# Two transformer layers on one core: whole-tile probability slots, 128-row tiles with a stacked tail in the first feed-forward product, and new due times

## The reference, cut to what matters

```python
def _layer(x, wqkv, qs, ksc, wo, lg, lb, w1, b1, w2, b2):
    h = shift_token(x)
    q, k, v = split(h @ wqkv)                  # 8 heads of 64
    q, k = rotary_xpos(l2norm(q) * qs, l2norm(k) * ksc)
    o = local_attention(q, k, v)               # window 128: own and previous 128 keys
    x = x + o @ wo
    h = layernorm(shift_token(x)) * lg + lb
    a, g = split(h @ w1 + b1)                  # 2 x 682 columns
    x = x + (a * gelu(g)) @ w2 + b2            # HID = 682
```

## Time and profile before

| what | value |
|---|---|
| median of 3 runs | 2306.94 us (2294.31 to 2309.14) |
| profiled execution | 2307.74 us, its span 2305.5 us |
| PE busy | 2047.1 us, 89% of the span |
| DVE busy | 1714.5 us, 74% |
| POOL busy | 1532.9 us, 66% |
| ACT busy | 1315.3 us, 57% |
| mean granted TensorE clock | 0.945 |

### The profile page before, as it was taken

The page is one execution under the profiler, slowest core; times in us unless marked ns, Lnnn a source line. Parts: engine busy times, 40 slices in busy tenths (PEclk is TensorE's granted clock), DMA queues, the critical chain, the costliest instruction groups (busy, mean ns, idle before and its releaser), DMA issues. The chain is left out here.

```text
span 2305.5 us, 45315 instructions
## 1 busy us (share of the span) xinstructions
PE 2047.1 (89%) x15360; PEld 1606.3 (70%) x15360; DVE 1714.5 (74%) x3132; ACT 1315.3 (57%) x3178; POOL 1532.9 (66%) x1401
## 2 busy tenths in 40 slices
PE   6579999999899999999998788979998989899985
PEld 4467777777677777777777576767676767677764
DVE  5587777677777887777676248888788788888883
ACT  3356566656665676567665356555655556456541
POOL 2465566556645755666465128988888789888984
PEclk7789999999999999999999889999999999999998
DMA  8343333333333333333333206777678767777685
GB/s 271 102 100 93 92 87 77 94 88 94 76 93 91 99 91 91 88 89 77 80 91 81 91 25 151 184 197 196 163 187 204 182 165 195 203 179 180 177 206 140
DMA packets 189280, 298.18 MB, mean 129 GB/s; under 512 B 52265, under 2 KB 97149, under 8 KB 188029
## 3 DMA queue, kind: packets, MB, share of 16 engines
q1 hardware_dynamic: 171388, 254.91, 43.1%
q10 hardware_dynamic: 10752, 21.51, 3.7%
q0 software_dynamic: 6912, 18.89, 3.2%
HBM read 56.04 MB, written 20.97 MB: 33 GB/s over the span
## 5 line engine op out<-in xcount | busy, mean ns | idle before, releaser
L2043 POOL TENSOR_TENSOR g_ring<-g_ring,g_rl 128x768 f32<-128x768 f32 (+6 forms) x168 | 384.8, 2304 | 40.7 <-DVE g_rl L1984 35.8
L1872 ACT ACTIVATE g_ring<-ps,g_mx 128x128 f32<-128x128 f32 (+7 forms) x384 | 274.2, 727 | 200.3 <-DVE g_mx L1966 92.2
L1759 PE MATMUL ps<-g_turned,g_latV 128*64 128x256 f32 (+1 forms) x1984 | 294.3, 442 | 73.6 <-issue 40.5
L855 ACT ACTIVATE l_pp<-ps,l_mx 128x256 f32<-128x256 f32 (+1 forms) x512 | 229.2, 464 | 169.0 <-DVE l_mx L992 169.0
L1131 POOL TENSOR_TENSOR l_pp<-l_pp,l_rl 128x1024 f32<-128x1024 f32 (+1 forms) x128 | 229.8, 1796 | 88.4 <-DVE l_rl L1000 88.2
L1991 DVE STREAM_TRANSPOSE g_ring<-g_ring 128x896 f32<-128x896 f32 (+4 forms) x264 | 257.2, 998 | 13.8 <-POOL g_ring L2043 13.5
L1759 PEld LDWEIGHTS ps<-g_turned,g_latV 128*64 128x64 f32 x1984 | 149.4, 143 | 162.9 <-issue 99.3
L1148 POOL TENSOR_TENSOR l_act_lo<-l_u,l_act_hi 114x512 fp32r<-114x512 f32 x96 | 125.5, 1307 | 162.4 <-ACT l_act_hi L905 162.2
L992 DVE CUSTOM_DVE_ANT_0 ps<-ps,l_mask 128x256 f32<-128x256 f32 (+1 forms) x512 | 188.4, 443 | 7.8 <-PE ps L704 7.8
L110 PE MATMUL ps<-l_wqkv_hi,l_x_hi 128*128 128x512 f32 x384 | 168.0, 437 | 17.9 <-POOL l_x_lo L1101 12.9
L110 PE MATMUL ps<-l_h_hi,l_w_hi 128*114 128x512 f32 (+1 forms) x384 | 160.7, 418 | 25.0 <-DVE l_h_lo L1049 22.2
(11 more groups left out here) (201 smaller groups left out, 6251.0 us busy)
## 6 DMA issues: line engine op xcount, KB each, us to landing
l_pt<-l_bt SPq DMA_DIRECT2D x1024, 64.0 KB, 2.0
g_turned<-g_ring SPq DMA_DIRECT2D x192, 112.0 KB, 3.0
g_turned<-g_ring SPq DMA_DIRECT2D x140, 128.0 KB, 3.8
g_turned<-g_pt SPq DMA_DIRECT2D x140, 128.0 KB, 3.5
g_turned<-g_ring SPq DMA_DIRECT2D x184, 96.0 KB, 2.9
g_turned<-g_ring SPq DMA_DIRECT2D x192, 80.0 KB, 2.4
g_turned<-g_pt SPq DMA_DIRECT2D x96, 96.0 KB, 2.2
l_tab<-turns SPq DMA_DIRECT2D x64, 128.0 KB, 2.1
```

Of the source, the lines that this page charges most:

```text
L855: act.activation(PP[:, i % NP, at, 0:n], ps[:, bank + a, jj * 2 * P:jj * 2 * P + n], ACT.Exp, bias=mx[:, g % 2, h, at:at + 1], scale=-1.0, ...
L1759: last = pe.matmul(o, latV[:, b % 2, c, :], turned[:, :, a, c, :, :], start=(c == 0), stop=(c == t), skip_group_check=True)
L1872: act.activation(to, some, ACT.Exp, bias=mx[:, u % 2, at:at + 1], accum_out=sm[:, u % 2, at:at + 1]).then_inc(s["ex"], 1)
L2043: pool.tensor_tensor(view, view, some, ALU.mult).then_inc(s["scaled"], 1)
```

## The change

Three edits in `layers`, and a new table.

1. `l_pp` and `l_bt` go. In their place there is `l_pb` with two slots, each of a whole tile. `exps` writes the probabilities in the order of the blocks, `scale` and `blocks` work in place. `exps` of tile `g` now waits, once, for the DMAs of `move(g-2)`; `blocks` waits for `scale` alone.
2. The feed-forward's tiles have 128 columns, so of 682 there are five full tiles and a rest of 42. The rests of both halves stand in one stationary operand (columns 0 to 41 and 64 to 105, zeros between), so the first product's last tile is one product of six matmuls into one bank, and the first product has 11 tiles where it had 12. In the second product the rest's high part stands in rows 0 to 41 and its low part in rows 64 to 105, over two copies of the 42 rows of `w2`, so that each of its two output halves takes two matmuls where it took three. The low part of the rest is written by DVE (`tail`), no longer by POOL.
3. The pieces of `w1` are split in two parts each (640 columns and the rest), the last piece of `w2` has its rest loaded and split twice, and three small memsets blank the padding.
4. All of `DUE` is new, but for the `bring` rows.

```diff
-HW = -(-HID // HT)
+HW = P
 HREM = HID - (HT - 1) * HW
+HMAIN = (HT - 1) * HW
+UPPER = slice(DH, DH + HREM)
...
-        PP = sb("l_pp", [P, NP, 4, 2 * P])
-        BT = sb("l_bt", [P, NB, 2, 4, 2, SQ])
+        PB = sb("l_pb", [P, 2, NB, 2, 4, 2, SQ])
...
                 def up(q, j, bank):
...
+                    if j == HT - 1:
+                        f = slice(2 * HMAIN, 2 * HMAIN + DH + HREM)
+                        three(pe, ps[0:DH + HREM, bank, :], [(W1_hi[:, k, f], W1_lo[:, k, f], hh[:, k, :], hl[:, k, :])
+                                                             for k in range(KD)]).then_inc(s["upg"], 1)
+                        return
...
                 def down(q, j, bank):
...
-                    pe.wait_ge(s["ulo"], n + 1)
+                    if j == HT - 1:
+                        pe.wait_ge(s["tail"], q + 1)
+                    else:
+                        pe.wait_ge(s["ulo"], (HT - 1) * q + j + 1)
...
+                        if j == HT - 1:
+                            pe.matmul(ps[:, bank + m, :], W2_hi[0:DH + HREM, j, f], ah[0:DH + HREM, j % NA, :], start=False,
+                                      stop=False)
+                            last = pe.matmul(ps[:, bank + m, :], W2_lo[0:mj, j, f], ah[0:mj, j % NA, :], start=False, stop=True)
...
                 def exps(g, h, bank):
...
-                    if i >= NP:
-                        act.wait_ge(s["blocks"], i - NP + 1)
...
                     if g >= 2:
                         act.wait_ge(s["rl"], i - 3)
+                        if h == 0:
+                            act.wait_ge(s[f"pt{g % 2}"], MOVED * (g // 2))
...
                 def blocks(g, h):
...
-                    if g:
-                        dve.wait_ge(s[f"pt{(g - 1) % 2}"], MOVED * ((g + 1) // 2))
-                    dve.transpose(BT[:, :, h, :, 0:n // P, :].rearrange("p j a r q -> p a r j q"),
-                                  PP[:, i % NP, :, 0:n].rearrange("p a (r j q) -> p a r j q", j=NB, q=SQ)
-                                  ).then_inc(s["blocks"], 1)
+                    view = PB[:, g % 2, :, h, :, 0:n // P, :].rearrange("p j a r q -> p j a (r q)")
+                    dve.transpose(view, view).then_inc(s["blocks"], 1)
...
+                def tail(q):
+                    j = HT - 1
+                    dve.wait_ge(s["uhi"], HT * (q + 1))
+                    dve.tensor_tensor(ah[UPPER, j % NA, :], u[0:HREM, j % 2, :], ah[0:HREM, j % NA, :], ALU.subtract
+                                      ).then_inc(s["tail"], 1)
...
-            "split": -12.69, "norm": -11.35, "var": -3, "gate": (-2.44, -1.97, -1.53, -1.48, -1.23, -0.63),
-            "scale": (-9.75, -9.39)},
+            "split": -12.19, "norm": -11.15, "var": -3.11, "gate": (-2.17, -2.0, -1.52, -1.23, -1.11),
+            "scale": (-9.93, -9.87)},
```

More of the change, by code:

```diff
@@ L407 @@
+            "store": -20.4, "move": -28.59},
         "pe": {
-            "proj": -3.66, "val": -3.55, "turn": -2.22, "scores": (-1.88, -1.86), "weigh": 0.45, "wo": 4.61,
-            "mean": 5.08, "var": 5.31, "centre": 5.44, "up": (5.8, 5.92, 6.16, 6.59, 6.6, 7.04),
-            "down": (6.61, 7.05, 7.37, 7.82, 7.87, 8.09)},
+            "proj": -3.73, "val": -3.46, "turn": -2.32, "scores": (-1.91, -1.87), "weigh": 0.43, "wo": 4.37, "mean": 4.99,
+            "var": 5.23, "centre": 5.37, "up": (5.87, 6.0, 6.14, 6.6, 6.72, 7.03),
@@ L411 @@
+            "down": (6.65, 7.04, 7.29, 7.72, 7.8, 7.94)},
         "act": {
-            "split": -3.96, "proj": -3.23, "norm": -2.43, "val": -2.47, "turn": -1.76, "divide": 1.05, "mean": 5.63,
-            "var": 5.68, "centre": 5.89, "up": (6.24, 6.53, 6.74, 6.99, 7.05, 7.38),
-            "gate": (6.43, 6.63, 7.04, 7.18, 7.73, 8.04), "scores": (-1.28, -1.05)},
+            "split": -4.02, "proj": -3.19, "norm": -2.61, "val": -2.94, "turn": -1.95, "divide": 0.98, "mean": 5.5,
+            "var": 5.64, "centre": 6.0, "up": (6.38, 6.5, 6.64, 6.95, 7.18, 7.28),
@@ L415 @@
+            "gate": (6.6, 6.62, 6.74, 7.11, 7.92, 7.96), "scores": (-1.27, -1.08)},
         "dve": {
-            "bring": (-45.53, -20.84, -5.06, -2.53, -1.95, -1.58, 2.75, 6.91, -3.84, -3.8, -3.51, -3.49, 2.47,
-             2.76, 3.67, 3.72, 5.21, 5.57, 6.42, 6.8), "scores": (-1.3, -1.26), "proj": -3.03, "turn": -1.62,
-            "wo": 5.26, "mean": 5.44, "centre": 5.92, "up": (6.38, 6.54, 6.85, 7.06, 7.26, 7.66), "out": 8.55,
-            "share": (-1.14, -0.81), "blocks": (-0.51, -0.45), "divide": 1.32, "low": 5.98},
+            "bring": (-45.53, -20.84, -5.06, -2.53, -1.95, -1.58, 2.75, 6.91, -3.84, -3.8, -3.51, -3.49, 2.47, 2.76,
+               3.67, 3.72, 5.21, 5.57, 6.42, 6.8), "scores": (-1.32, -1.3), "proj": -3.08, "turn": -1.79, "wo": 4.99,
@@ L420 @@
+            "mean": 5.39, "centre": 5.89, "up": (6.22, 6.54, 6.84, 6.96, 7.23, 7.63), "out": 8.52, "share": (-1.18, -1.05),
+            "blocks": (-0.83, -0.45), "divide": 1.43, "low": 5.92, "tail": 8.19},
         "pool": {
-            "split": -12.69, "norm": -11.35, "var": -3, "gate": (-2.44, -1.97, -1.53, -1.48, -1.23, -0.63),
-            "scale": (-9.75, -9.39)},
+            "split": -12.19, "norm": -11.15, "var": -3.11, "gate": (-2.17, -2.0, -1.52, -1.23, -1.11),
+            "scale": (-9.93, -9.87)},
@@ L524, in layers @@
                        "chi clo wo xw xcol mean hc hsq var ve vl vr vn vn2 vn3 rs rsb hn hhi hlo upg upa ge u uhi ulo "
-                       "dn y out whi wlo")
+                       "dn y out whi wlo pad tail")
         def place_of(g):
@@ L773, in down @@
                         f = slice(m * P, (m + 1) * P)
[L774 to L775 removed]
+                        if j == HT - 1:
+                            pe.matmul(ps[:, bank + m, :], W2_hi[0:DH + HREM, j, f], ah[0:DH + HREM, j % NA, :], start=False,
+                                      stop=False)
+                            last = pe.matmul(ps[:, bank + m, :], W2_lo[0:mj, j, f], ah[0:mj, j % NA, :], start=False, stop=True)
+                        else:
+                            last = three(pe, ps[:, bank + m, :], [(W2_hi[:, j, f], W2_lo[:, j, f], ah[:, j % NA, :],
+                                                                   al[:, j % NA, :])], start=(j == 0), stop=False)
                     last.then_inc(s["dn"], 1)
@@ L893, in up @@
                     if j >= 2:
-                        act.wait_ge(s["ulo"], n - 1)
-                    act.activation(u[0:mj, j % 2, :], ps[0:mj, bank, :], ACT.Gelu, bias=b1c[0:mj, q // (B * NC), 1, j:j + 1]
+                        act.wait_ge(s["ulo"], (HT - 1) * q + j - 1)
+                    rows = UPPER if j == HT - 1 else slice(0, mj)
+                    act.activation(u[0:mj, j % 2, :], ps[rows, bank, :], ACT.Gelu, bias=b1c[rows, q // (B * NC), 1, j:j + 1]
                                    ).then_inc(s["ge"], 1)
@@ L1068, in _ @@
                 dve.memset(xw[:, 1, 0:1], 0.0).then_inc(s["xcol"], 1)
+                blank = slice(2 * HMAIN + HREM, 2 * HMAIN + DH)
+                for some in (W1_hi[:, :, blank], W1_lo[:, :, blank], W2_hi[32:DH, HT - 1, :]):
+                    dve.memset(some.bitcast(F32), 0.0).then_inc(s["pad"], 1)
+                dve.wait_ge(s["pad"], 3)
                 for e in flow.program["dve"]:
@@ L1091, in _ @@
                         low(e[1])
+                    elif e[0] == "tail":
+                        tail(e[1])
                     elif e[0] == "up":
```

82 lines of the change are left out of this document (40 added, 42 removed).

## The result

| | median us | lowest to highest | runs |
|---|---|---|---|
| before | 2306.24 | 2294.31 to 2314.13 | 20 |
| changed | 2293.13 | 2283.0 to 2309.97 | 20 |

The ratio is 0.9946, with a 95% interval of 0.993 to 0.9963: 12 to 13 us less, where 27.6 were forecast. Timed once more beside the experiments, the changed kernel had 0.9974 (0.9954 to 0.9994). I compare the experiments with the middle of the two, 0.996 (9 us), and keep in mind that the two differ by 0.003, which is 7 us.

The account below looks back on a forecast made before the run. PE was taken to bound the layers' steady part, busy 95% of it, with short waits around the layer norm. The terms -29.6 - 3 + 0 + 0 + 3 + 2 = -27.6 us, from 2306.94, gave 2279 us, range 2255 to 2303.

Parts of the forecast that it names:

- rival (a): Layer norm: ACT's and DVE's chain sets the period, half or more of 29.6 us returns as PE waits; 2293 us, 28%.
- Its term for the clock: Steady chunks: 73.0 us at granted clock 1.00, 77.0 at 0.96; a fall in half of them costs up to 32 us.
- The matmuls, -29.6: Feed-forward, last `up` and `down` tiles: 8 fewer matmuls in each of 16 chunks, 0.231 us each, 29.6 us off PE.
- The new order, 0: Around the layer norm: bank wait (13.1 us) goes, wait for the centred chunk grows by as much; 0 together.
- The probabilities in place, -3: Layers' attention: instruction prices unchanged, DVE's 14.9 us wait for DMAs before `blocks` goes; 3 us gained.
- The tail, 0: DVE's subtraction ahead of `l_qk_lo`: 0.69 to 3.3 us each, hidden by the `down` matmuls; 0, uncovered 53 us.
- The bank of the last `up` tile, +3: Last `up` tile takes a `turn` bank pair, cover fits by 0.2 us; 3 us cost, between 0 and 19.
- The start, +2: Before 185 us: two subtractions per `w1` piece and a longer POOL memset; 2 us cost, from 0 to 13.
- The second layer's pieces, 0: Second layer's `w1` pieces, split in two, lie beside full PE work; no cost.
- the 1.8 us of a chunk: Sign of a right forecast: a steady chunk of the layers shorter by about 1.8 us.
- the 953 us of the large attention: Sign of a right forecast: the large attention, left alone by the change, as long as before, 953 us.
- The sign for (a): Sum of PE's waits in the layers higher by 15 us or more, or steady granted clock below 0.97.

Follow-up runs that it names:

- the probabilities alone: The kernel before with only the probabilities in place, on its own due times (0.9985) and on the new ones with a sixth gate time (1.0049).
- the old table: The changed kernel on the due times of the kernel before, five POOL gate times and 8.2 for the tail: 2303.59 us, ratio 1.0004.

## Why the prediction was wrong

The forecast of 2279 us was 14 us too low. The value is that of rival (a), 2293, but by luck: its mechanism, half or more of the 29.6 us coming back as waits, is only a part of what happened. In a pair of chunks 2.15 us of the 3.7 were gained; 0.90 went because the remaining matmuls cost more, 0.65 as idle time of PE. Its term for the clock was also misread: the two chunks of the earlier trace rows are not of one kind but an odd and an even one, which differ by 1.0 us at the full clock (72.88 and 73.86), and a fall of the clock, which takes a chunk's mean from 1.00 to 0.98, costs 1.55 us; 0.96 is two of them. Eight more falls are 12 us, not 32. By the prediction's own steps:

- **The matmuls, -29.6.** The price of 0.231 us is right where PE sets the pace: 12 matmuls put back cost 2.76 us. The step that failed first is the price of the part in `down`. "I price a narrow one of 106 columns like the others" looked at the columns; the tail's `down` has operands of 42 and 106 *rows* in turn, and with the scores behind them four matmuls took 3.09 us where six had taken 3.10. Instead of 16 x 0.46 = 7.4 us this is nothing. Equal rows bring the starts from 0.37 to 0.44 us back to 0.23. The Trainium skill, TensorEngine Tiling (Array Packing), Key Properties, says that a change of tiling mode drains TensorE. It doesn't say that 42 rows beside 106 are such a change, and no run here shows that this is the reason.
- **The new order, 0.** This is the second step that failed. "I take 0 for both together" counted two waits around the layer norm and was right on these (-13.1 and +10.3 us). But PE's idle time rose by 0.65 us a pair, 5 us in 8 pairs. And the order has no price of its own: it costs 1.4 us a pair without the smaller tiles (15 us in the medians) and gives 1.15 with them, while the smaller tiles are worth 3.5 us a pair in the new order and 1.0 in the old one. I added terms that are not independent.
- **The probabilities in place, -3.** The prices are right (1.90, 0.48 and 1.23 us) and DVE's wait for the moves is gone, but the gain is not shown: 3.5 us in the medians, with an interval that includes none, and 0.0 in a pair of chunks at the full clock (146.77 against 146.74).
- **The tail, 0.** Right in a steady chunk, in part by luck: `l_qk_lo`, behind the tail, ends 0.14 us ahead of the scores, with 1.3 us forecast as the remaining cover and 1.31 us as the tail's price. The cover is there only because the four matmuls are slow; with 106 rows in each the scores wait for `l_qk_lo`, which is why a faster `down` brought so little. In the two chunks with weights the tail cost 5.6 us of waits, and taking them away changed nothing in the end.
- **The bank of the last `up` tile, +3.** No such wait is in the changed kernel's list: nothing. It is as near as the prediction had it (0.2 us of cover): with eight matmuls fewer ahead of it, PE waits 6.7 us for the low part of Q and K at an `up`, in 13 chunks.
- **The start, +2.** Mis-sized: 5 us. The second pair of each piece is some 3.5 of them, and the trace shows a cast caught behind POOL there. The new order has its share: the probabilities alone have their first `up` after 134.9 us on the old table and 136.1 on the new one, and on the old table the two parts cost nothing there (133.4).
- **The second layer's pieces, 0.** Right for the pieces: one part in place of two made that stretch no shorter. But the stretch as a whole gained nothing over the kernel before (313.8 us against 313.7), where two steady pairs would give 4; why is open.

With what was measured the sum is: matmuls -29.6 + 7.2, idle time in the pairs +5.2, start +5, the rest 0: -12 us. The median of the first comparison fell by 13.1 us, that of the second by 6, and the layers of the two profiles by 6.3 and 8.8. The large attention, 7 and 4 us longer in these two profiles than before, is one place where executions differ; that it makes the difference of the medians is not shown.

Of the signs named ahead, these were right: the counts of matmuls, the three prices, the bank wait gone and the wait for the centred chunk larger, PE fully busy in the feed-forward (36.00 of 36 us from 514 to 550). Wrong were the distance of 0.23 us, the 1.8 us of a chunk (1.1 at equal clocks) and the 953 us of the large attention (960.3 and 957.2). The sign for (a), a sum of PE's waits higher by 15 us or more, came to 13.4.

What stays open: why the new order costs 1.4 us a pair when the tiles are twelve. Its list of waits has larger entries for the centred chunk and for Q and K, and one that no other version here has:

```profile
PE ps L110 <- POOL l_act_lo L1144: 6.1, 14, 2.7
```

That is PE in `down`, waiting for POOL's low part. The sixth gate time there was my choice, and no run varied it, so some of these 6 us may be the choice and not the order. The same holds for the tail's due time on the old table.

## What to carry to other kernels

When one change takes work off the busiest engine and also sets the order anew, the terms are not to be added: measure or argue each edit on both orders, since in the old one most of the freed time can be lost (1.0 us of 3.7 a pair was kept here). Compare stretches of the same work at the same granted clock before comparing medians; here the pair of chunks told 2 us of 147 where medians of 12 runs could tell 5 of 2300. Then hold the count against the whole stage: pairs and start promised 12 us here, and the layers' first and last matmuls showed 6 and 9. And ask of a removed instruction what its neighbours look like afterwards: those that remain in another shape can cost as much as the two that went.

## What the runs showed of the hardware that was not expected

- Matmuls of 512 columns with 42 and 106 rows in turn start 0.37 to 0.44 us apart, those of 106 rows alone 0.23 (0.30 behind the first).
- A cast of 128x42, with one input, took 1.88 us beside a POOL instruction of 2.37 us and ended with it. The Trainium skill, GPSIMD Engine Reference, Key points, counts VectorE's 2-port modes among what contends with GpSimd; that this cast ran in one is not shown here.
- The clock's falls came at the same chunks in two profiles of the changed kernel, but for the last chunks, and at others in kernels that differ from it in one small edit. A fall costs an even chunk 1.55 us (72.38 to 73.93), so one more or less in each of 16 chunks is 25 us, more than most edits tried here.
